# First attention batch of a fused network kernel: prepared by token tile and by row half, with its scores placed between the head stacks

## What is computed

```
scale, shift = jnp.split(emb @ W_emb + b_emb, 2, axis=-1)
xn = _rms_norm(x, g_norm) * (1.0 + scale) + shift
q, k, v = heads of xn @ W_qkv
q = _rms_norm(q, g_q);  k = _rms_norm(k, g_k)
attn = softmax(einsum('bhqd,bhkd->bhqk', q, k) * d ** (-0.5))
o = einsum('bhqk,bhkd->bhqd', attn, v)
return o + o @ W_out
```

## Time and profile before

| | us |
|---|---|
| median of 3 executions | 1719.85 (1718.77 to 1723.79) |
| profiled execution, its own time | 1705.28 |
| span of its trace | 1703.5 |
| busy: PE | 1550.3 (91%) |
| busy: DVE | 1186.9 (70%) |
| busy: ACT | 900.8 (53%) |
| busy: POOL | 609.3 (36%) |

### The profile page before, as it was taken

How to read it: one execution, slowest core, us unless ns; L and a number is a source line. 1 busy time by engine, 2 the same in 40 slices (tenths; PEclk the granted TensorE clock), 3 DMA queues, 4 the chain that set the end, 5 groups by cost and what they waited for, 6 DMA issues and landing times.

```text
span 1703.5 us, 76387 instructions
## 1 busy us (share of the span) xinstructions
PE 1550.3 (91%) x31935; PEld 1205.0 (71%) x31935; DVE 1186.9 (70%) x4287; ACT 900.8 (53%) x3329; POOL 609.3 (36%) x1821
## 2 busy tenths in 40 slices
PE   7999999999999999999549996778888888999999
PEld 6999999999999999999426563345655655544444
DVE  6788888787877778888665543677777777672231
ACT  6555555555555556554515554477777778431230
POOL 0333333333333333333435554343445443560000
PEclk9999999999999999955559997789999998999999
DMA  4200101101110011110435744000000010220001
GB/s 182 55 27 8 52 21 34 38 16 54 42 39 5 18 47 45 47 32 17 139 116 167 250 137 161 26 1 26 26 2 2 2 57 2 73 76 31 19 1 50
DMA packets 45735, 91.28 MB, mean 54 GB/s; under 512 B 6608, under 2 KB 25168, under 8 KB 45392
## 3 DMA queue, kind: packets, MB, share of 16 engines
q1 hardware_dynamic: 39152, 65.94, 12.2%
q0 software_dynamic: 6240, 20.45, 3.6%
HBM read 67.69 MB, written 18.61 MB: 51 GB/s over the span
## 4 chain that ended last, share of the span: by engine, by line
PE 31%; ACT 7%; DVE 6%; POOL 3%; issue 2%; DMA 2%; SPq 0%; ACTq 0%; POOLq 0%; DVEq 0%
PE bank L1290 9%; PE bank L1176 5%; PE bank L1368 4%; PE bank L1100 4%; PE bank L1122 2%; POOL arena L2101 2%; ACT arena L1517 2%; ACT arena L1522 2%; PE bank L1194 1%; PE bank L1089 1%; PE bank L1271 1%; DVE arena L1906 1%; DMA hrows<-arena 1%; PE bank L1247 1%; DMA arena<-hrows,arena 1%
## 5 line engine op out<-in xcount | busy, mean ns | idle before, releaser
L412 PE MATMUL bank<-arena 128*128 128x8 f16 x12288 | 500.0, 170 | 8.6 <-issue 4.0
L415 PE MATMUL bank<-arena 128*128 128x16 f16 x12288 | 495.4, 182 | 1.0 <-issue 0.6
L412 PEld LDWEIGHTS bank<-arena 128*128 128x128 f16 x12288 | 410.8, 97 | 37.6 <-ACT bank L509 20.3
L415 PEld LDWEIGHTS bank<-arena 128*128 128x128 f16 x12288 | 411.7, 97 | 2.1 <-issue 1.2
L676 POOL TENSOR_TENSOR arena<-arena 128x16 f32<-128x16 f32 x512 | 117.8, 230 | 524.7 <-DVE arena L619 510.6
L479 ACT ACTIVATE arena<-arena 128x16 f32<-128x16 f32 x512 | 114.6, 224 | 305.0 <-DVE arena L598 304.6
L609 DVE TENSOR_TENSOR_SCAN arena<-arena,bank 128x64 f32<-128x64 f32 x512 | 146.8, 287 | 17.9 <-ACT arena L479 2.6
L598 DVE TENSOR_REDUCE arena<-bank 128x16 f32<-128x48 f32 x512 | 100.0, 195 | 79.9 <-PE bank L415 75.0
L1290 PE MATMUL bank<-arena 128*128 128x512 f16 x704 | 153.6, 379 | 0.0
L385 PE MATMUL bank<-arena 128*128 128x256 f16 x1008 | 147.6, 273 | 1.4 <-issue 1.4
L1176 PE MATMUL bank<-arena 128*128 128x512 f16 x576 | 138.6, 393 | 4.0 <-DVE arena L1861 3.8
(11 more groups left out here) (209 smaller groups left out, 2671.9 us busy)
## 6 DMA issues: line engine op xcount, KB each, us to landing
arena<-yrows SPq DMA_DIRECT2D x16, 512.0 KB, 4.2
arena<-in_wgu SPq DMA_DIRECT2D x48, 128.0 KB, 2.2
arena<-in_wdn SPq DMA_DIRECT2D x8, 512.0 KB, 3.9
hrows<-arena SPq DMA_DIRECT2D x16, 256.0 KB, 4.0
arena<-in_xtok SPq DMA_DIRECT2D x16, 256.0 KB, 9.5
out_y<-arena SPq DMA_DIRECT2D x16, 256.0 KB, 2.0
arena<-in_wih SPq DMA_DIRECT2D x4, 768.0 KB, 7.5
arena<-in_whh SPq DMA_DIRECT2D x4, 768.0 KB, 10.4
```

The lines of the kernel that those rows point to most:

```text
L412: mm = nc.tensor.matmul(dst[:, j * B:(j + 1) * B, 1], w, h[:, 0], start=home not in opened, stop=False, skip_group_check=True)
L415: mm = nc.tensor.matmul(dst[:, j * B:(j + 1) * B, 1:3], w, h.rearrange("p a c -> p c a"), start=home not in opened, stop=False, skip_group ...
```

## The change

Nothing that is computed changes. Batch 0 is prepared in smaller parts.

- Token tile 0 is turned into two banks (`turn_bank(0, k)`: pieces 0 and 1 in bank 4, 2 and 3 in bank 2). DVE adapts two pieces of it and ACT the other two. Its high and low halves are made for the tile alone, and `project(0, 0)` and `project(0, 1)`, which use tile 0 only, come before tiles 2 and 3 are turned. Tile 1 is adapted and split behind it.
- `root` and `invert` over four row halves become `first_root(i)` and `first_invert(i)` for one each, and the steps of the halves are laced.
- One stack is made before the scores; the other three stand before heads 2, 6 and 10 (`STACK_FIRST`).
- The high half of batch 1 (`norm_x(1, ...)`) and the adapting of tile 3 move behind the split of batch 0. Counts of semaphores follow: tile 0 now counts twice in `xnf_done`, and batch 0 gives four counts of `rmsk_done` and `rk_done`.

```diff
--- before.py
+++ after.py
@@ -888,8 +888,9 @@
             return range(SUMMED + 2 * b, min(SUMMED + 2 * b + 2, NG))
-        def turn_bank(g):
-            return bank[4 + 3 * (g % 2)]
+        def turn_bank(g, k=0):
+            return bank[2] if g == 0 and k >= 2 else bank[4 + 3 * (g % 2)]
         KC = SX * SX
@@ -905,6 +906,7 @@
         NORM_X_AT = {9: 0, 10: 1}
+        STACK_FIRST = {2: 1, 6: 2, 10: 3}
         vzero = sem("vzero")
@@ -1152,16 +1154,19 @@
                     if g >= 2:
-                        pe.wait_ge(xnf_done, g - 1)
+                        pe.wait_ge(xnf_done, g)
                     for k in range(KT):
-                        mm = nc.tensor.transpose(turn_bank(g)[:, k * P:(k + 1) * P],
+                        mm = nc.tensor.transpose(turn_bank(g, k)[:, k * P:(k + 1) * P],
                                                  unit_x[g % 2][:, k * P:(k + 1) * P], ident)
...
                 def project(b, i, first=False):
-                    if i == 0:
+                    if i == 0 and not first:
                         pe.wait_ge(xn_lo, KT * (b + 1))
+                    elif i in (0, 2) and first:
+                        pe.wait_ge(xn_lo, KT // 2 * (i // 2 + 1))
                     if i < 2 and not first:
@@ -1302,7 +1307,7 @@
                         if h in OUT_AT and len(turned_in(b)) > 0:
-                            pe.wait_ge(xnf_done, EARLY + 2 * b + 1 + OUT_AT[h])
+                            pe.wait_ge(xnf_done, EARLY + 2 * b + 2 + OUT_AT[h])
                         if not last:
@@ -1335,15 +1340,17 @@
                 turn_back(0)
                 turn_back(1)
                 project(0, 0, True)
+                project(0, 1, True)
                 turn_back(2)
-                project(0, 1, True)
+                project(0, 2, True)
                 turn_back(3)
-                for i in range(2, 6):
+                for i in range(3, 6):
                     project(0, i, True)
-                for g in range(4):
-                    stack(0, g)
-                pe.wait_ge(xnf_done, EARLY)
+                stack(0, 0)
+                pe.wait_ge(xnf_done, EARLY + 1)
                 for h in range(H):
+                    if h in STACK_FIRST:
+                        stack(0, STACK_FIRST[h])
                     scores(0, h, True)
                 pe.wait_ge(vzero, 3)
@@ -1469,15 +1476,20 @@
                 def turned(g):
-                    b, half = divmod(g, 2)
                     act.wait_ge(turn_mm, g + 1)
-                    for k in range(KT):
-                        op = A.activation(xnf[:, b, k, half * P:(half + 1) * P], turn_bank(g)[:, k * P:(k + 1) * P],
-                                          ACT.Identity, scale=ada[:, 0, k, b:b + 1], bias=ada[:, 1, k, b:b + 1])
+                    for k in range(2 - 2 * g, KT):
+                        op = A.activation(xnf[:, 0, k, g * P:(g + 1) * P], turn_bank(g, k)[:, k * P:(k + 1) * P],
+                                          ACT.Identity, scale=ada[:, 0, k, 0:1], bias=ada[:, 1, k, 0:1])
                     op.then_inc(xnf_done, 1)
+                def high_tile(g):
+                    act.wait_ge(xnf_done, g + 2)
+                    A.activation(xn[:, 0, :, g * P:(g + 1) * P], xnf[:, 0, :, g * P:(g + 1) * P], ACT.Copy)\
+                        .then_inc(xn_hi, 1)
                 def norm_x(b, half):
-                    act.wait_ge(xnf_done, 2 * b + 2)
+                    act.wait_ge(xnf_done, 2 * b + 3)
                     A.activation(xn_half(0, half), xnf_half(b, half), ACT.Copy).then_inc(xn_hi, 1)
@@ -1489,6 +1501,12 @@
                     A.activation(rmsk[:, :, :], ssk[:, :, :], ACT.Sqrt, scale=1 / DH, bias=epsb[:, :])\
+                        .then_inc(rmsk_done, 1)
+                def first_root(i):
+                    act.wait_ge(ssk_done, i + 1)
+                    A.activation(rmsk[:, i, :], ssk[:, i, :], ACT.Sqrt, scale=1 / DH, bias=epsb[:, :])\
                         .then_inc(rmsk_done, 1)
@@ -1580,30 +1598,39 @@
                     root_rows(g)
                 unit_rows(0)
                 unit_rows(1)
+                turned(0)
+                high_tile(0)
                 turned(1)
-                norm_x(0, 0)
-                norm_x(0, 1)
+                high_tile(1)
                 for g in (2, 3):
                     square_rows(g)
                     root_rows(g)
                 unit_rows(2)
+                take_out(0, 0)
                 unit_rows(3)
-                take_out(0, 0)
                 take_out(0, 1)
-                for g in (4, 5):
-                    square_rows(g)
-                    root_rows(g)
+                square_rows(4)
+                root_rows(4)
+                first_root(0)
+                high_qk(0, 0)
                 take_out(0, 2)
+                first_root(1)
+                square_rows(5)
+                root_rows(5)
+                high_qk(0, 1)
                 take_out(0, 3)
-                root(0)
+                first_root(2)
                 take_out(0, 4)
+                high_qk(0, 2)
+                first_root(3)
+                high_qk(0, 3)
                 take_out(0, 5)
-                for n in range(4):
-                    high_qk(0, n)
+                stack(0, 0)
+                stack(0, 1)
                 norm_x(1, 0)
                 norm_x(1, 1)
-                for g in range(4):
-                    stack(0, g)
+                stack(0, 2)
+                stack(0, 3)
                 turn_max(0)
                 high_v(0)
                 for g in turned_in(0):
@@ -1850,25 +1877,30 @@
                     dve.wait_ge(turn_mm, g + 1)
-                    for k in range(KT):
+                    for k in range(KT if g > 0 else 2):
                         op = V.tensor_scalar(xnf[:, b, k, half * P:(half + 1) * P], turn_bank(g)[:, k * P:(k + 1) * P],
...
                     op.then_inc(xnf_done, 1)
-                def norm_x(b):
-                    for half in range(2):
-                        dve.wait_ge(xn_hi, 2 * b + half + 1)
-                        V.tensor_tensor(xn_half(1, half), xnf_half(b, half), xn_half(0, half),
-                                        ALU.subtract).then_inc(xn_lo, KT // 2)
+                def norm_x(g):
+                    dve.wait_ge(xn_hi, g + 1)
+                    V.tensor_tensor(xn[:, 1, :, g * P:(g + 1) * P], xnf[:, 0, :, g * P:(g + 1) * P],
+                                    xn[:, 0, :, g * P:(g + 1) * P], ALU.subtract).then_inc(xn_lo, KT // 2)
                 def sum_squares(b, i):
...
                 def invert(b):
-                    dve.wait_ge(rmsk_done, b + 1)
+                    dve.wait_ge(rmsk_done, b + 4)
                     V.reciprocal(rk[:, :, :], rmsk[:, :, :]).then_inc(rk_done, 1)
-                    dve.wait_ge(rk_done, b + 1)
+                    dve.wait_ge(rk_done, b + 4)
+                def first_invert(i):
+                    dve.wait_ge(rmsk_done, i + 1)
+                    V.reciprocal(rk[:, i, :], rmsk[:, i, :]).then_inc(rk_done, 1)
+                    dve.wait_ge(rk_done, i + 1)
                 def normalise_qk(b, i):
@@ -1983,29 +2015,38 @@
                 for g in range(2):
                     invert_rows(g)
                 adaptive(0)
+                norm_x(0)
                 residual(2)
-                norm_x(0)
+                norm_x(1)
                 residual(3)
-                for g in (2, 3):
-                    invert_rows(g)
-                for g in (2, 3):
-                    adaptive(g)
+                invert_rows(2)
+                invert_rows(3)
                 sum_squares(0, 0)
                 residual(4)
+                first_invert(0)
+                normalise_qk(0, 0)
                 sum_squares(0, 1)
+                low_qk(0, 0)
+                adaptive(2)
+                invert_rows(4)
+                first_invert(1)
+                normalise_qk(0, 1)
                 residual(5)
-                invert_rows(4)
+                sum_squares(0, 2)
+                low_qk(0, 1)
+                first_invert(2)
+                normalise_qk(0, 2)
                 invert_rows(5)
-                sum_squares(0, 2)
                 sum_squares(0, 3)
-                invert(0)
-                for i in range(4):
-                    normalise_qk(0, i)
-                for n in range(4):
-                    low_qk(0, n)
-                for g in range(4):
-                    stack(0, g)
+                low_qk(0, 2)
+                first_invert(3)
+                normalise_qk(0, 3)
+                low_qk(0, 3)
+                adaptive(3)
+                stack(0, 0)
                 for h in range(H):
+                    if h in STACK_FIRST:
+                        stack(0, STACK_FIRST[h])
                     maximum(0, h)
                 low_v(0)
                 for b in range(B - 2):
```

## The result

The changed kernel took 1706.84 us (median of 4 executions, 1704.33 to 1709.43), the kernel before 1721.05 beside it (4 executions, 1718.77 to 1723.79). The ratio is 0.9925, 95% interval 0.9907 to 0.9943: 14.2 us less on the medians, where 5.6 were forecast. Four later comparisons of the same two kernels gave 0.9942, 0.994, 0.996 and 0.9949. Two later executions of the kernel before, of 3175.54 and 2172.76 us (beside e13 to e15 and beside e18), count as slow and are in no ratio.

What follows compares the result with a forecast made beforehand. The prediction took the chain of waits through ACT, DVE and POOL, not PE, to bound the touched stretch. 3.1 us before the first stack plus 2.5 behind it gave 5.6, so 1719.85 - 5.6 = 1714.2 us, range 1710.5 to 1718.8.

Steps and rivals of the forecast that it cites:

- Up to the first projection: First row transpose to first projection in batch 0: the projection starts at 1048.3, 2.2 us earlier.
- The halves of q and k: Projections and q/k steps up to the first stack transpose: it starts at 1072.4 instead of 1075.50, 3.1 us earlier.
- the three charged waits: DVE steps on q and k waiting for POOL: 1.5 us in all (0.5 + 0.5 + 0.55).
- The slower rival: DVE and POOL port waits in the laced q/k steps: up to 11.4 us on top, 1725.6 us; chance 0.04.
- Stacks and scores: First stack to maxima's transpose: 3.1 + 13.2 = 16.3 us instead of 18.85, 2.5 us less.
- the rival in which it does not rise: Clock stays low in the laced stacks: 15.9 us from first score to maxima's transpose, gain 3 us, 1716.9; chance 0.20.
- the sum: Whole forecast gain up to `project(1, 0)`: 3.1 us before the first stack and 2.5 behind it, together 5.6 us.
- Behind the maxima: `project(1, 0)` after the maxima's transpose: starts at 1088.9 at the low clock like before, with no further gain.
- The median of the runs stands 14.6 us above the profiled execution: Base of the forecast time: this difference was carried over, giving 1719.85 - 5.6 = 1714.2 us.

Runs made afterwards that it cites:

- e13: Changed kernel with ACT and DVE steps reordered, residuals of tiles 4 and 5 ahead of the first sum over heads: 1704.43 us, ratio 0.9945 to the kernel before.
- e15: The kernel before, unchanged, run again against itself: 1714.09 us, ratio 1.0002.
- e18: The kernel of e16 again on another chip, beside the kernel before: 1698.64 us against 1710.09, ratio 0.993.
- e2: The changed kernel again, unmodified, beside the kernel before: 1704.78 us, ratio 0.9942.
- e8: The changed kernel once more, unmodified, beside a kernel before at 1709.37 us: ratio 0.994.
- e17: The changed kernel again, unmodified, run beside e16 and the kernel before: 1705.86 us, ratio 0.9949.
- e3: The kernel before with only the lacing of stacks and scores added: 1710.51 us, ratio 0.9969 to the kernel before.
- e11: The kernel before padded with 2 tiny ACT and 8 tiny DVE instructions in idle time ahead of the attention: ratio 0.9995.
- e14: The changed kernel again, unmodified, beside the kernel before: 1707.65 us, ratio 0.996.
- e6: The changed kernel padded with 16 tiny ACT and 16 tiny DVE instructions ahead of the attention: ratio 0.9952 to the kernel before.
- e10: The changed kernel padded with 5 tiny ACT and 1 tiny DVE instructions ahead of the attention: ratio 0.9962 to the kernel before.
- e12: The changed kernel padded with 2 tiny ACT and 8 tiny DVE instructions ahead of the attention: ratio 0.9965 to the kernel before.
- e16: e13 with DVE's adapting of tile 2 behind the fourth low half and the last sum ahead of the third: 1704.31 us, ratio 0.9937 to the kernel before.

## Why the prediction was wrong

The prediction's times are those of a trace whose T is 1044.78, so they are read here from T.

**Up to the first projection: right.** T + 3.5, as predicted, in all eight traces (3.47 to 3.48).

**The halves of q and k: right.** First stack predicted at T + 27.6, found at 27.1 to 27.8, mean 27.4; before it was 30.7 (seven traces), so 3.2 us are gained against 3.1. The pieces hold one by one: the reciprocal of 16 columns taken at 0.25 takes 0.25, the root taken at 0.29 takes 0.29, ACT's wait for tile 5 taken at 3.5 us is 3.67, and DVE meets POOL as feared. The residual of tile 4 at 1.26 us (shown above) and the normalisings of the second and third half at 1.26 and 1.25 instead of 0.68 are the three charged waits. Each stands beside a POOL instruction that began 0.55 to 0.57 us before it; DVE and then POOL, changed kernel:

```profile
1072.45 1.26 DVE L1909 SCALAR_TENSOR_TENSOR arena<-arena 128x512 f32<-128x512 f32 x1
...
1077.04 1.25 DVE L1909 SCALAR_TENSOR_TENSOR arena<-arena 128x512 f32<-128x512 f32 x1
```

```profile
1065.22 1.27 POOL L2137 TENSOR_TENSOR arena<-arena,gg 128x512 f32<-128x512 f32 x1
...
1071.90 1.26 POOL L2137 TENSOR_TENSOR arena<-arena,gg 128x512 f32<-128x512 f32 x1
1076.47 1.27 POOL L2133 TENSOR_TENSOR arena<-arena 128x512 f32<-128x512 f32 x1 [3.31 <-ACT arena L1498]
```

Each of the three ends 0.55 us after the POOL instruction beside it. The Trainium skill ("SBUF — State Buffer", section "Who interferes with whom") has the mechanism, a port pair held for a whole instruction, and these rows agree (1.26 us instead of 0.68). A fourth wait, in tile 1's low half (1.20 instead of 0.69), stood beside PE's work and cost nothing. The slower rival did not happen: the other DVE instructions ran at their own length. It was POOL that took longer, 1.25 to 1.27 us instead of 1.04 for three of its four squares.

**Stacks and scores: mis-sized, because in six of eight traces the clock went the other way.** The forecast had the clock rise in the laced stacks and 13.2 us from first score to maxima's transpose. e2 and e8 show just that (13.15 in both). In the six others the clock was high at the first stack, fell within 1 us of its end and stayed low through nearly all the lacing; there it took 15.3 to 15.7 us, near the price that I had put on the rival in which it does not rise (15.9, chance 0.20). So from the first stack to the maxima's transpose the eight traces gain 1.2 us on average (17.5 against 18.8) where the sum has 2.5. The rival's total, a gain of 3 us, was wrong all the same: the first stack at the high clock brings the first score 2.3 us behind it in the changed trace instead of 3.1, and more is gained behind the maxima. The clock in stretches of 6 us (time; length; PE, PEld, DVE, ACT, POOL busy; clock; DMA share and GB/s), changed kernel and then e2, whose T is 7.2 us earlier and whose stretches are set 6 us earlier:

```profile
1082.00:1088.00 6.00, 4.39 (x40) 3.72 (x40) 4.31 (x10) 1.56 (x2) 0.00 (x0) 0.62 0.00 0
1088.00:1094.00 6.00, 5.10 (x33) 3.34 (x32) 4.97 (x8) 2.53 (x4) 4.93 (x6) 0.50 0.01 3
1094.00:1100.00 6.00, 4.85 (x28) 2.45 (x26) 5.04 (x9) 1.02 (x1) 0.06 (x1) 0.50 0.00 0
```

```profile
1076.00:1082.00 6.00, 4.34 (x32) 3.39 (x31) 3.45 (x7) 2.26 (x3) 0.00 (x0) 0.55 0.00 0
1082.00:1088.00 6.00, 4.21 (x48) 3.07 (x48) 6.00 (x11) 2.86 (x4) 4.99 (x6) 1.00 0.01 3
1088.00:1094.00 6.00, 4.40 (x17) 1.61 (x18) 4.31 (x7) 2.53 (x5) 0.00 (x0) 0.80 0.01 1
```

e2 has its maxima's transpose 2.1 us sooner behind T, and yet 1.7 us more from T to the end: from the first exponential to the end e2 and e8 take 606.1 and 605.8 us, five of the six others 601.8 to 602.5 (e17 has 605.0). The laced kernels suggest that a dip of the clock in the stacks is one that is not had later: the four traces in which the clock rises in the lacing (e2, e8, e3, e13) are all of the long kind, seven of the eight others of the short one. The kernel before shows that the dip does not decide it. It has the same two kinds, 602.8 to 603.3 in three traces and 606.1 to 606.2 in four, and its own trace (603.3) and e11 (606.2) have the same dips up to the first exponential: 6.8 us low from T + 27.8 and T + 27.7 on, 13.7 us low from T + 41.5 and T + 41.2 on. The two kinds differ in the loop, where the clock is low for 51.2 to 54.6 us in the shorter three and for 58.0 to 61.4 in the longer four. So the clock costs 2.2 to 2.6 us in the stacks themselves, near the 2.7 of the prediction (15.9 against 13.2); why the total does not show it, and what decides between the two kinds, is open.

**Behind the maxima: 2.3 us that the sum does not have.** I had `project(1, 0)` at the low clock as before, 5.32 us. It takes 4.3 to 4.6 in the eight changed traces, since the clock is back up within it. The first exponential is 5.4 us earlier on average (T + 49.9 against 55.3) though the maxima's transpose is only 4.5 earlier, and from it to the end 603.5 us stand against 604.8. About 0.6 of these 1.3 us are the share of the two kinds among the traces (four of seven are long before, three of eight after). From T to the end this sums to 653.4 against 660.1 us: 6.7 us, or 6.1 and 6.7 within the short and the long kind. The sum of 5.6 was 1.1 too small, and that it was no further off is luck: 1.2 too much in the stacks stand against 2.3 too little behind them.

**The step that failed: "The median of the runs stands 14.6 us above the profiled execution for reasons that this trace doesn't show; I carry the difference over".** The difference does not belong to the kernel. Six later medians of the kernel before, on other chips or at other times, are 1715.43, 1709.37, 1713.69, 1713.19, 1714.83 and 1710.09, mean 1712.8. Against that the profiled execution was 7.5 us short (1705.28) and the three timed ones 7.0 us long (1719.85, above all six). In the trace the shortness lies before T, which is at 1044.8 where its six copies have 1052.5 on average; 5.0 us of it are in the GRU, 785.4 against 788.1 to 795.0. Of the three timed executions there is no trace. So the predicted 1714.2 was 7.4 us too high, and 7.0 of that is the base: with the mean base the same sum gives 1707.2. That this comes so near to the measured 1706.84 is in part luck again, as the gain was under-sized (by 1.1 us in the traces) and the changed kernel was somewhat long in that comparison too: its later medians are 1704.78, 1701.12, 1707.65 and 1705.86, mean 1704.9.

**The other part of the 14.2 us.** Over the seven later comparisons the new lists have a mean ratio of 0.9953 against 1.0000 for the six of the old ones, 8.1 us; the traces have 6.7 us behind T and 1.0 before it, and T scatters by about 4 us from one trace to the next, so that the 1.0 can't be told from nothing. The first comparison's 14.2 us (9.8 to 16.0 by its interval) stay unexplained by some 2 us at the least. In it the kernel before was 8.3 us above the mean of its later medians and the changed one 2.0. It is one of five pairs, and an interval over the runs of one sitting doesn't hold what differs between sittings; whether some other thing made the kernel before slow in that one is open.

## What to carry to other kernels

Measure a change from an instruction that both traces share, ahead of the first moved one, and leave what lies before it out of the account: here two spans differed by 4 us in the wrong direction while the touched part was 6 us shorter. A predicted *time* is no better than the base that it is subtracted from, and a base of three executions with a spread of 5 us beside a profiled one 15 us lower was a warning that the range should have taken in. Where two identical kernels differ by as much as a predicted gain, single traces can't confirm how a gain divides into its parts. And when lists are laced, look first for the step that waits for nothing and stands ahead of one that does: moving such steps (a residual, an adapting) out of the chain, with their neighbours, was worth about half of the change again (3.3 us by the ratios beside 8.1, 4.6 by the traces beside 6.7).

## What the runs showed of the hardware

- The same GRU of 12288 products, which no edit touches, ran in 783.8 to 795.5 us over 20 traces, with the median product at 169 or 170 ns in all of them. The ranges of old and new lists, of padded and plain kernels and of the chips all overlap, so none of these sets it alone; what does is open.
- The clock's dips around the stacks differ between traces of the changed kernel and its padded copies: low for 6.8 and 3.4 us in e2 and e8, for 13.7 and 3.4 in e14 and e17, and for 20.5 us in one piece in the changed trace, e6, e10 and e12. The Trainium skill ("TensorE: Matmul & The Clock Gate", section "What's actually happening") has the point at which the clock rises vary by 500 ns either way; these traces show it vary by more, with the rise behind the first projection at T + 6.3 to 8.8 though the projection starts at T + 3.5 in all eight.
- From the first exponential to the end the same loop takes about 603 or about 606 us, also where the clock's dips were the same up to there (603.3 in before, 606.2 in its padded copy e11).
- DVE's reads of PSUM kept their own length beside POOL: four maxima took 2.53 us in e2 while POOL worked, six took 3.73 without it (0.63 and 0.62 each). A COPY within the arena waited in part: 0.58 instead of 0.29 us in e16, at the end of POOL's gain.
